# State-space prelude reordered: x projections first, taps read from PSUM, diagonals through DRAM, one residual moved to VectorE

## The chip, the cores and the metric

The kernel runs on 1 core of one Trainium2 chip. Its time is the device time of one execution in microseconds (us), from the first instruction to the last. Below, "batch 0" and "batch 1" are the two sequences of the input; all arithmetic here is fp32.

## The reference

Two layers, each a mixer and a mixture of experts, with adaptive layer norms around them. What the change touches is the first mixer, a state-space block over two sequences of 1024 tokens, 256 wide, 512 inner channels, 16 states, cut here to its core:

```
xz = h @ in_proj.T;  x, z = split(xz)                 # 512 + 512 channels
x = silu(conv over 4 taps of x, causal, + conv_b)
dt, B, C = split(x @ x_proj.T)                        # 16, 16, 16 columns
dt = softplus(dt @ dt_proj.T + dt_b)
h_t = h_(t-1) * exp(dt * A[n]) + dt * x * B_t[n]      # for 16 states n
y_t = sum over n of C_t[n] * h_t[n];   y = (y + x * D) * silu(z)
out = y @ out_proj.T
```

and, in the second layer's experts, `out = h + moe(rmsnorm(h))`, followed by `x = x + gb * out`. The term `gb * h` of that sum is the residual that the change moves to another engine.

## The kernel before, in words

The program is one sequence of stages: `modulation`, `mamba`, `moe` (layer 0), two attention stages, `moe` (layer 1). Each stage is a block with one hand-written instruction stream per engine; semaphores are its only ordering, so the order of calls in each stream is the schedule. Tiles have 128 partitions; 512 inner channels are CD = 4 chunks of 128 by L = 1024 tokens. The first number in a call like `conv(b, k)` is the batch and the second the chunk; the changed file numbers them i = 4b + k.

`mamba` has a prelude and a recurrence.

- **Prelude.** VectorE (DVE) normalises the rows of a batch (L424) and applies scale and shift (L427, L428). TensorE (PE) transposes them (`turned`, L652), ScalarE (ACT) copies the result out of PSUM to `hT` (`rows_of`, L522). PE makes the products of `projected` (L665), 16 half-chunks per batch: first the four x chunks, then the four z chunks; batch 0's z come ahead of batch 1's x. ACT copies each x half to `xp` (L536) and writes the fourth tap to `xc` (L541). `conv` on DVE adds the other three taps from `xp` (L433), `activated` (L527) makes silu of it: `xa`. `narrow` (L675) multiplies `xa` by `x_proj`; `split_xd` copies dt, B, C (L442). `steps` on PE (L693) makes the step sizes, `relu` (DVE, L452) and `absolute` (ACT, L561) their two halves, `falling` (Exp, L566) and `log1p` (Ln, L571) the softplus; `steps` on DVE sums them (L458) and multiplies by `xa` to `u` (L461).
- **What goes to DRAM.** `xa`, `z`, `dt`, `u` of each chunk (0.5 MB each) and the B and C rows are spilled by SyncE (SP), and read back before use. SP's stream is in program order: a wait in it holds all DMA issues behind it. For batch 0 the C values become 16 diagonal blocks `dg` of 128x1024 on GpSimd (POOL, L628), from columns that PE has transposed (L682); for batch 1 `place_words` (L342) writes the C values, 4 bytes each, onto the diagonals of a zeroed 8 MB table in DRAM (8 DMAs of 16x128 values, filled with zeros by L297), and `load_diag` (L369) reads that table back during the recurrence.
- **Recurrence.** 128 iterations, at = 16 kk + n, for 8 chunks kk of 16 states n. ACT: `decay` writes exp(dt A) to PSUM (L608). POOL: `dbx` = u times the broadcast B row, `bb` (L638; `load_rows`, L364). DVE: one scan (L496) over 1024 tokens into `h`. PE transposes `h` (L725) and sums over the states by a product with the diagonal block (L740). The first scans need `bb[0]` to be back from DRAM, the first sum needs `dg[0]`.

In `moe` of layer 1 POOL runs four instructions at the start (L925, L927: `res = hs * gb`, `x = x + res`, two groups of four rows). At the same time DVE finishes the statistics of the norm (`norm.spread`, L1286 to L1295), then waits for the norm's weights `nwb` (DMA, L882) and scales the rows (L1133).

Names of areas: `bb` and `dg` are 16 slots of 128x1024 each, `ud` four such slots, `xz`, `h`, `dbx`, `hts` two each. The prelude's temporaries lie in them: before the recurrence may load `bb[n]` or `dg[n]`, the temporary in that slot has to be done.

Of the kernel before, what the change touches and what calls it, by code (L numbers as in the profile page):

```python
# [7 lines left out]
P = 128  # L8
# [213 lines left out]
def mamba(nc, g, w_in, conv_w, conv_b, xproj, dtw, dtb, a_log, dskip, w_out):  # L222
    ctx = ExitStack()
    with ctx:
# [16 lines left out]
        ct = sb("ct", [P, TB * NS])  # L241

        xn = bb[:, 0:2, :].rearrange("p a (t d) -> p (a t) d", d=D)
        hT = [bb[:, 2:4, :], bb[:, 4:6, :]]
        win = bb[:, 6:8, :]
        xa = [bb[:, 8:12, :], bb[:, 12:16, :]]
        dtv, abs_v = [bb[:, 0:4, :], bb[:, 4:8, :]], [dg[:, 12:16, :], bb[:, 8:12, :]]
        zeros = dg[:, NS - 1, :]
        words = ud[:, :, :, :].rearrange("p a b l -> p (a b l)")
        XPW = L + DC - 1  # L250
        xp = words[:, 0:2 * XPW].rearrange("p (a l) -> p a l", a=2)
        wx = words[:, 2 * L + 64:2 * L + 64 + CD * 80].rearrange("p (k n) -> p k n", k=CD)
        wdt = words[0:DTR, 3 * L:3 * L + DI]
        xc, zr = h[:, :, :], xz[:, :, :]
# [28 lines left out]
        def dt_pair(b, k):  # L283

            return (3, 2, 0, 1)[k] if b == 1 else 3

        @block.sync
        def _(sp):
# [10 lines left out]
            def spill_z(b, k):  # L299
                sp.wait_ge(s_z, 2 * (b * CD + k) + 2)  # L300
                sp.dma_start(d_z[b * CD + k], zr[:, k % 2, :]).then_inc(s_zout[k % 2], 16)

            def spill_xa(b, k):
                sp.wait_ge(s_xa, b * CD + k + 1)
                sp.dma_start(d_xa[b * CD + k], xa[b][:, k, :]).then_inc(s_xaout[b], 16)

            def spill_rows(b):
                sp.wait_ge(s_xd, b + 1)
                sp.dma_start(d_b[b], xd[b][64:80, :]).then_inc(s_bout, 16)
                if b == 1:  # L310
                    sp.dma_start(d_c, xd[b][32:48, :]).then_inc(s_cout, 16)
# [2091 lines left out]
```

## Time and profile before

| | us |
|---|---|
| median of 3 runs (lowest, highest) | 2559.26 (2557.56, 2559.46) |
| the profiled execution | 2562.03 |
| its span, first to last instruction in the profile | 2560.2 |

The profile is one execution; times of its rows count from the start of the span. Whether something is on the path to the end of this single-core program is read stage by stage: the stages follow each other, and what an early stage ends sooner moves all later ones.

### The profile page before, as it was taken

The page shows a single profiled execution, that of the slowest core. Times are in us where ns is not written, and L with a number is a line of the kernel's source. Part 1 is how long each engine was busy: PE and PEld are TensorE (multiplying, and loading weights), DVE is VectorE, ACT ScalarE, POOL GpSimd, SP SyncE. Part 2 cuts the span into 40 slices and gives each one's busy share as a digit, 9 for nine tenths or more (in the row PEclk, how much of TensorE's full clock was granted, in tenths as well). Part 3 has the DMA queues.
Part 4 walks back from the last instruction along what each step waited for, and adds up shares of the span by engine and source line. Part 5 has one row for each costly group of instructions (what it writes and reads, how often), then busy time and mean ns, then how long its engine had stood idle before and what let it go on. Part 6 is the DMA issues. An engine that isn't in the chain of part 4 may idle for free. (4 is left out here: it accounts for less than half of the span.)

```text
span 2560.2 us, 34038 instructions
## 1 busy us (share of the span) xinstructions
PE 2337.4 (91%) x12526; PEld 1769.7 (69%) x12526; DVE 1416.2 (55%) x2477; ACT 1120.5 (44%) x1913; POOL 1140.2 (45%) x665
## 2 busy tenths in 40 slices
PE   6959999985999995999998989999999999949997
PEld 2329999983777764998896667777776777725554
DVE  5658888866222223545665875556556555463332
ACT  3467777722111112434433555546456464521221
POOL 0439999920332321433454445454545535223442
PEclk8969999997999997999998999999999999969999
DMA  6274181118412212000000100000000001055223
GB/s 243 83 284 114 58 329 59 64 73 267 133 30 34 32 26 98 1 1 1 1 1 19 56 1 19 15 10 19 1 23 1 19 9 34 1 175 145 45 42 64
DMA packets 108244, 168.30 MB, mean 66 GB/s; under 512 B 30482, under 2 KB 77586, under 8 KB 106004
## 3 DMA queue, kind: packets, MB, share of 16 engines
q1 hardware_dynamic: 93108, 145.35, 16.3%
q0 software_dynamic: 14976, 20.78, 5.1%
q8 instruction: 105, 1.72, 0.3%
q14 instruction: 55, 0.45, 0.1%
HBM read 115.94 MB, written 52.32 MB: 66 GB/s over the span
## 5 line engine op out<-in xcount | busy, mean ns | idle before, releaser
L638 POOL TENSOR_TENSOR mb_dbx<-mb_ud,mb_bb 128x1024 f32<-128x1024 f32 x128 | 302.0, 2363 | 57.2 <-DVE mb_h L496 41.7
L496 DVE TENSOR_TENSOR_SCAN mb_h<-ps,mb_dbx 128x1024 f32<-128x1024 f32 x128 | 292.2, 2289 | 47.9 <-ACT ps L608 37.5
L2298 PE MATMUL ps<-a_eT,a_v 128*128 128x512 f32 x576 | 297.2, 598 | 3.9 <-ACT a_eT L2175 3.9
L2131 POOL TENSOR_TENSOR a_e<-a_e,a_rc 128x1024 f32<-128x1024 f32 (+5 forms) x144 | 188.9, 1321 | 248.3 <-DVE a_rc L2047 247.9
L946 POOL DMA_INDIRECT e_acc<-e_hid,e_ids x78 | 123.6, 1585 | 370.8 <-DVE e_hid L1240 354.4
L2057 DVE TENSOR_REDUCE a_mx<-ps 128x1 f32<-128x1024 f32 (+7 forms) x256 | 192.7, 753 | 159.1 <-PE ps L2277 158.3
L2175 ACT ACTIVATE a_eT<-ps 128x512 f32<-128x512 f32 x288 | 171.1, 594 | 245.3 <-PE ps L2288 244.6
L740 PE MATMUL ps<-mb_dg,mb_hts 128*128 128x128 f32 x2048 | 251.2, 276 | 0.4
L740 PEld LDWEIGHTS ps<-mb_dg,mb_hts 128*128 128x128 f32 x2048 | 240.0, 193 | 1.9 <-issue 1.9
L1226 DVE COPY e_work<-ps 128x256 f32<-128x256 f32 x78 | 33.2, 425 | 356.4 <-PE ps L1064 356.4
L1803 POOL TENSOR_TENSOR a_elo<-a_e,a_ehi 128x1024 fp32r<-128x1024 f32 x48 | 117.6, 2451 | 223.2 <-ACT a_ehi L1656 117.7
L2159 ACT ACTIVATE a_e<-ps,a_nb 128x1024 f32<-128x1024 f32 (+5 forms) x192 | 156.0, 813 | 79.7 <-DVE a_nb L2058 72.9
L1095 PE MATMUL ps<-e_wd,e_work 128*128 (+1 forms) x780 | 189.0, 384 | 1.9 <-ACT e_work L994 1.9
L988 ACT ACTIVATE e_hid<-ps 128x688 f32<-128x688 f32 (+1 forms) x78 | 52.3, 670 | 299.8 <-PE ps L1076 299.8
L1076 PE MATMUL ps<-e_wg,e_work 128*128 x468 | 178.2, 518 | 4.7 <-issue 1.6
L617 ACT ACTIVATE mb_hts<-ps 128x512 f32<-128x512 f32 x256 | 139.3, 595 | 92.4 <-PE ps L725 92.4
L1076 PE MATMUL ps<-e_wu,e_work 128*128 x468 | 170.5, 500 | 0.0
L2274 PE MATMUL ps<-h_qkhi,h_wmhi 128*128 128x512 f32 (+3 forms) x288 | 152.7, 530 | 12.1 <-ACT a_e L2159 5.3
L725 PE MATMUL ps<-ident,mb_h 128*128 128x128 f32 x1024 | 135.4, 276 | 29.5 <-DVE mb_h L496 29.4
L1095 PEld LDWEIGHTS ps<-e_wd,e_work 128*128 128x128 f32 (+1 forms) x780 | 138.9, 190 | 30.0 <-issue 15.8
L2288 PE MATMUL ps<-ident,a_e 128*128 128x128 f32 x992 | 151.2, 275 | 8.2 <-DVE hs L2104 5.9
L2115 POOL TENSOR_TENSOR x<-x 128x1024 f32<-128x1024 f32 x35 | 91.0, 2601 | 135.8 <-DVE x L2090 135.8
(377 smaller groups left out, 5310.9 us busy)
## 6 DMA issues: line engine op xcount, KB each, us to landing
mb_bb<-mb_db_rows SPq DMA_DIRECT2D x16, 1024.0 KB, 12.6
mb_ddiag<-mb_dg SPq DMA_DIRECT2D x1, 8192.0 KB, 22.3
mb_dg<-mb_ddiag SPq DMA_DIRECT2D x8, 1024.0 KB, 14.0
e_wg<-in_g SPq DMA_DIRECT2D x8, 688.0 KB, 10.4
e_wu<-in_u SPq DMA_DIRECT2D x8, 688.0 KB, 10.7
e_wd<-in_d SPq DMA_DIRECT2D x8, 640.0 KB, 10.7
mb_dxa<-mb_bb SPq DMA_DIRECT2D x8, 512.0 KB, 2.6
mb_dz<-mb_xz SPq DMA_DIRECT2D x8, 512.0 KB, 2.9
```

Source lines behind the costliest of these rows:

```text
L496: dve.tensor_tensor_scan(h[:, at % 2, :], pair(at % 2), dbx[:, at % 2, :], 0.0, ALU.mult, ALU.add).then_inc(s_h, 1)
L638: pool.tensor_tensor(dbx[:, at % 2, :], ud[:, kk % 2, 0, :], bb[:, n, :], ALU.mult).then_inc(s_dbx, 1)
L740: mm = pe.matmul(ps[:, 6 + half, q * P:(q + 1) * P], hts[:, at % 2, c:c + P], dg[:, n, c:c + P], start=(n == 0 and q == 0), stop=(n == NS ...
L1076: mm = pe.matmul(ps[:, b0 + a, 0:FN], xT[:, i % 2, k * P:(k + 1) * P], w[:, ds(e), k, a * FN:(a + 1) * FN].rearrange("p a n -> p (a n)"), ...
L1095: mm = pe.matmul(ps[:, 6, 0:D], hT[0:n, i % 2, c * P:(c + 1) * P], wd[0:n, ds(e), c, :].rearrange("p a n -> p (a n)"), start=(c == 0), sto ...
L2057: own(dve.reduce_max(mx[:, q:q + 1], pair(n, (i + 1) * P), AX_X))
L2131: pool.tensor_tensor(probs(i, h), probs(i, h), rc[:, q:q + 1].to_broadcast([P, (i + 1) * P]), ALU.mult).then_inc(s["en"], 1)
L2159: act.activation(probs(i, h), pair(n, (i + 1) * P), ACT.Exp, bias=nb[:, q:q + 1], scale=SCALE, accum_out=sm[:, q:q + 1]).then_inc(s["e"], 1)
L2175: act.activation(eT[:, k % ER, :], ps[:, bank[what, u, i, h], :], ACT.Copy).then_inc(s["eT"], 1)
L2274: mm = pe.matmul(ps[:, o + t, 0:c1 - c0], qT[x_][j][:, i * P:(i + 1) * P], kT[y_][:, c0:c1], start=(x_ == y_), stop=(x_ == LO and not last))
L2288: tr = pe.transpose(ps[:, bank[token], h * P:(h + 1) * P], probs(i, h, j * P, (j + 1) * P), ident[:, :])
L2298: mm = pe.matmul(ps[:, 6 + rows[u, i] % 2, :], v[:, j, u % 2, :], eT[:, k % ER, :], start=(j == 0), stop=(j == i))
```

## The change

In `mamba`:

- Scale and shift leave DVE: PE transposes them to columns (`columns`), DVE copies these (`modT`), and ACT applies them in the eviction of the transposed rows.
- PE makes all x chunks first, with both narrow products between; batch 0's z come next, batch 1's z last, behind batch 1's step sizes. PSUM is handed out in four pairs of banks by the table `PAIR`.
- The copy `xp` is gone: ACT's tap and DVE's three taps read the product in PSUM.
- POOL's 16 diagonal products, the C columns and their copies are gone. `place_words` runs for both batches: for batch 0 in SP's prelude, for batch 1 behind all of batch 0's diagonal loads. `load_diag` runs for batch 0 too, 8 loads of 1 MB.
- Chunk 0's `dt` and `u` stay in `ud`; the first load of `ud` is gone.
- `z` has eight places: two of them are `dbx`, two are `h` (chunks 4 and 5). The first `dbx` waits for z 2 and 3 to be in DRAM, the first scan for z 4 and 5.

In `moe` of layer 1 the four residual instructions run on DVE, ahead of its wait for the logits.

```diff
-        zeros = dg[:, NS - 1, :]
+        zeros = dbx[:, 0, :]
+        zr = [xz[:, 0, :], xz[:, 1, :], dbx[:, 0, :], dbx[:, 1, :], h[:, 0, :], h[:, 1, :], xz[:, 0, :], xz[:, 1, :]]
...
+        PAIR = {"x": (2, 3, 0, 2, 3, 0, 2, 3), "dt": (1, 0, 1, 0, 2, 1, 0, 3), "z": (3, 1, 0, 3, 2, 1, 0, 3), "narrow": (1, 2)}
...
+            for k in range(CD):
+                spill_xa(0, k)
+            spill_xa(1, 0)
+            spill_rows(0)
+            spill_xa(1, 1)
+            place_words(0)
+            spill_xa(1, 2)
+            spill_xa(1, 3)
+            spill_z(0)
+            spill_z(1)
+            sp.wait_ge(s_tr, 4)
+            sp.wait_ge(s_dgout, 16 * TB)
+            load_diag(0, 0)
+            spill_z(2)
+            spill_z(3)
+            sp.wait_ge(s_ip, BK + CD)
+            load_diag(0, 1)
+            spill_rows(1)
+            for k in range(1, CD):
+                spill_steps(0, k)
+            sp.wait_ge(s_u, CD)
+            sp.wait_ge(s_bout, 16 * B)
+            load_rows(0, 0)
+            load_rows(0, 1)
+            sp.wait_ge(s_dtout[0], 16 * (CD - 1))
+            load_rows(0, 2)
+            load_rows(0, 3)
...
+            load_rows(0, 4)
+            load_rows(0, 5)
+            spill_steps(1, 0)
+            spill_steps(1, 1)
+            spill_z(4)
+            spill_steps(1, 2)
+            spill_z(5)
+            spill_steps(1, 3)
+            sp.wait_ge(s_log, BK)
+            sp.wait_ge(s_sp, BK)
+            load_diag(0, 2)
+            load_diag(0, 3)
...
             load_xz(0)
-            place_words()
+            for q in range(NS // 2):
+                sp.wait_ge(s_dgin[q], 16)
+            place_words(1)
...
-                    ins = dve.scalar_tensor_tensor(xc[:, k % 2, :], xp[:, k % 2, tap:tap + L], cw[:, k, tap:tap + 1],
-                                                   xc[:, k % 2, :], ALU.mult, ALU.add)
+                    late = DC - 1 - tap
+                    ins = dve.scalar_tensor_tensor(xc[:, i % 2, late:L], pair(PAIR["x"][i])[:, 0:L - late], cw[:, k, tap:tap + 1],
+                                                   xc[:, i % 2, late:L], ALU.mult, ALU.add)
...
+                if at == 0:
+                    dve.wait_ge(s_zout[2], 32)
                 if at >= 2:
                     dve.wait_ge(s_tp, 2 * (at - 1))
                 dve.tensor_tensor_scan(h[:, at % 2, :], pair(at % 2), dbx[:, at % 2, :], 0.0, ALU.mult, ALU.add).then_inc(s_h, 1)
...
+                if at == 0:
+                    pool.wait_ge(s_u, 1)
+                    pool.wait_ge(s_zout[1], 32)
...
-                if kk == CD and n % 2 == 0:
-                    pe.wait_ge(s_dgin[n // 2], 16)
+                if kk % CD == 0 and n % 2 == 0:
+                    pe.wait_ge(s_dgin[n // 2], 16 * (kk // CD + 1))
```

On SP, the place of the placed words (`mb_dxa` are spills of xa, `mb_dz` of z, `mb_ddt` and `mb_du` of dt and u; `mb_ddiag<-mb_dc_rows` are the placed words, `mb_bb<-mb_db_rows` the B rows, `mb_dg<-mb_ddiag` the diagonals). Before:

```order
L315 DMA mb_ddt<-mb_bb 128x1024
L317 DMA mb_du<-mb_bb 128x1024
L315 DMA mb_ddt<-mb_bb 128x1024
L317 DMA mb_du<-mb_bb 128x1024
L364 DMA mb_bb<-mb_db_rows 128x2048 x6
L349 DMA mb_ud<-mb_du 128x1024
L350 DMA mb_ud<-mb_ddt 128x1024
L357 DMA mb_xz<-mb_dxa 128x1024
L358 DMA mb_xz<-mb_dz 128x1024
L342 DMA mb_ddiag<-mb_dc_rows 16x128x1 x8
L349 DMA mb_ud<-mb_du 128x1024
```

Changed:

```order
L308 DMA mb_dxa<-mb_bb 128x1024 x4
L308 DMA mb_dxa<-mb_dg 128x1024
L312 DMA mb_dc_rows<-mb_hts 16x1024
L313 DMA mb_db_rows<-mb_hts 16x1024
L308 DMA mb_dxa<-mb_dg 128x1024
L327 DMA mb_ddiag<-mb_dc_rows 16x128x1 x8
L308 DMA mb_dxa<-mb_dg 128x1024 x2
L304 DMA mb_dz<-mb_xz 128x1024 x2
L362 DMA mb_dg<-mb_ddiag 128x2x1024
L304 DMA mb_dz<-mb_dbx 128x1024 x2
L362 DMA mb_dg<-mb_ddiag 128x2x1024
```

The eight placed-word DMAs stood behind all loads of B rows and the first loads of `ud` and `xz`; now they stand behind six spills of xa and the first C and B rows, and every spill of z, dt and u and every load of the recurrence is behind them.

Further down the same stream of the changed kernel, up to the spill of z 5:

```order
L356 DMA mb_bb<-mb_db_rows 128x2048 x6
L317 DMA mb_ddt<-mb_dg 128x1024
L319 DMA mb_du<-mb_dg 128x1024
L317 DMA mb_ddt<-mb_dg 128x1024
L319 DMA mb_du<-mb_dg 128x1024
L304 DMA mb_dz<-mb_h 128x1024
L317 DMA mb_ddt<-mb_dg 128x1024
L319 DMA mb_du<-mb_dg 128x1024
L304 DMA mb_dz<-mb_h 128x1024
```

The two `mb_dz<-mb_h` are z 4 and z 5, which the first scan waits for; six loads of B rows and six spills of dt and u stand ahead of the second.

In the second expert stage, POOL before:

```order
L1830 UNCONDITIONAL_BRANCH
L919 UNCONDITIONAL_BRANCH
L925 TENSOR_TENSOR e_scr<-hs,mod 128x1024
L927 TENSOR_TENSOR x<-x,e_scr 128x1024
L925 TENSOR_TENSOR e_scr<-hs,mod 128x1024
L927 TENSOR_TENSOR x<-x,e_scr 128x1024
L932 DMA e_xin<-e_rows,e_ids 128x264 x5
```

and DVE in the changed kernel, behind the scaled rows (L1170 is L1133 of the file before):

```order
L1170 SCALAR_TENSOR_TENSOR raw<-hs,n_rstd,e_nwb 128x256 x8
L1174 CAST raw<-e_cst 128x128
L1175 CAST raw<-e_cst 128x128
L1176 TENSOR_TENSOR e_gbd<-mod 128x256
L1177 MEMSET e_first 128x1
L1189 TENSOR_TENSOR e_scr<-hs,mod 128x1024
L1191 TENSOR_TENSOR x<-x,e_scr 128x1024
L1189 TENSOR_TENSOR e_scr<-hs,mod 128x1024
L1191 TENSOR_TENSOR x<-x,e_scr 128x1024
L1196 COPY e_hid<-ps 128x128
```

The four 128x1024 instructions stood at the head of POOL's stream, beside DVE's statistics, and stand now on DVE behind the scaled rows, ahead of the copy of the logits.

## Rows read from the trace of the kernel before

**Rows 1.** The page, part 1: busy time, share of the span, instructions of each engine.

```profile
PE 2337.4 (91%) x12526; PEld 1769.7 (69%) x12526; DVE 1416.2 (55%) x2477; ACT 1120.5 (44%) x1913; POOL 1140.2 (45%) x665
```

**Rows 2.** Timeline, 34 to 226 us: start us, us, engine, line, out<-in, count, [idle before].

```profile
42.33 0.26 ACT L514 ACTIVATE mb_am<-mb_am 128x64 f32<-128x64 f32 x1 [6.34 <-DMA mb_ud<-in_dtw]
...
51.58 0.34 PEld L665 LDWEIGHTS ps<-mb_bb 128*128 128x128 f32 x1 [0.52 <-issue]
...
52.74 0.19 PEld L665 LDWEIGHTS ps<-mb_bb 128*128 128x128 f32 x1 [0.24 <-issue]
...
95.02 1.22 DVE L442 COPY mb_hts<-ps 80x1024 f32<-80x1024 f32 x1 [23.88 <-PE ps L675]
...
179.80 4.46 DVE L496 TENSOR_TENSOR_SCAN mb_h<-ps,mb_dbx 128x1024 f32<-128x1024 f32 x2
185.85 4.47 DVE L496 TENSOR_TENSOR_SCAN mb_h<-ps,mb_dbx 128x1024 f32<-128x1024 f32 x2 [1.58 <-ACT ps L608]
...
199.03 2.29 DVE L496 TENSOR_TENSOR_SCAN mb_h<-ps,mb_dbx 128x1024 f32<-128x1024 f32 x1 [0.57 <-ACT ps L608]
...
225.63 2.29 DVE L496 TENSOR_TENSOR_SCAN mb_h<-ps,mb_dbx 128x1024 f32<-128x1024 f32 x1 [0.37 <-ACT ps L608]
```

**Rows 3.** Stretch 45 to 51 us: length, busy us of PE, PEld, DVE, ACT, POOL, granted clock, DMA.

```profile
45.00:51.00 6.00, 5.27 (x12) 2.83 (x11) 4.49 (x9) 1.60 (x4) 0.00 (x0) 0.50 1.03 416
```

**Rows 4.** Groups by line, 34 to 180 us: engine, operation, shapes, count | busy us, mean ns | idle.

```profile
L665 PE MATMUL ps<-mb_bb 128*128 128x512 f32 x128 | 66.1, 672 | 10.1 <-ACT mb_xz L551 8.2 <-issue 1.9
...
L693 PE MATMUL ps<-mb_hts,mb_ud 16*128 16x512 f32 x32 | 19.2, 747 | 2.9 <-ACT mb_dg L561 2.9
...
L452 DVE TENSOR_SCALAR mb_bb<-ps,mb_db 128x1024 f32<-128x1024 f32 x8 | 10.2, 1279 | 7.3 <-PE ps L693 7.3
...
L458 DVE TENSOR_TENSOR mb_bb<-mb_bb,mb_dg 128x1024 f32<-128x1024 f32 x4 | 4.9, 1220 | 3.3 <-ACT mb_dg L571 3.3
...
L522 ACT ACTIVATE mb_bb<-ps 128x512 f32<-128x512 f32 x8 | 4.5, 601 | 1.9 <-PE ps L652 1.8
```

**Rows 5.** Line 433 on VectorE, 50 to 75 us, then 98 to 125 us.

```profile
L433 DVE SCALAR_TENSOR_TENSOR mb_h<-mb_ud,mb_cw,mb_h x12: 1279/1285/1285, 55.3 to 69.9; 128x1024 f32<-128x1024 f32 x12
...
L433 DVE SCALAR_TENSOR_TENSOR mb_h<-mb_ud,mb_cw,mb_h x11: 1286/2814/2818, 97.5 to 123.3; 128x1024 f32<-128x1024 f32 x11
```

**Rows 6.** SyncE's DMA issues, 170 to 240 us, and landing times of line 342.

```profile
186.62 47.74 SPq L342 DMA_DIRECT2D mb_ddiag<-mb_dc_rows  x8
...
DMA to landing us min/median/max: 14.1/16.6/26.7
```

**Rows 7.** The page, part 6: DMA issues, count, KB each, us from issue to landing.

```profile
mb_ddiag<-mb_dg SPq DMA_DIRECT2D x1, 8192.0 KB, 22.3
```

**Rows 8.** DMA packets of all queues, 186 to 202 us, then 205 to 241 us.

```profile
DMA packets 1153, 6.68 MB, mean 418 GB/s; under 512 B 126, under 2 KB 126, under 8 KB 551
...
DMA packets 14105, 0.12 MB, mean 3 GB/s; under 512 B 14100, under 2 KB 14100, under 8 KB 14100
```

**Rows 9.** Timeline of the second expert stage's start, and the landing of line 882.

```profile
2248.72 2.34 POOL L925 TENSOR_TENSOR e_scr<-hs,mod 128x1024 f32<-128x1024 f32 x1 [33.70 <-POOLq L1830]
2248.73 2.35 DVE L1286 TENSOR_TENSOR n_mean<-n_st 128x8 f32<-128x8 f32 x1 [0.32 <-PEq L1830]
...
2249.56 0.46 SPq L882 DMA_DIRECT2D e_nwb<-in_n  x1
...
2251.12 0.17 DVE L1287 TENSOR_TENSOR n_t<-n_st 128x8 f32<-128x8 f32 x1
...
2251.32 2.19 DVE L1288 SCALAR_TENSOR_TENSOR n_t<-n_t 128x8 f32<-128x8 f32 x1
...
2258.77 3.25 DVE L1133 SCALAR_TENSOR_TENSOR raw<-hs,n_rstd,e_nwb 128x256 f32<-128x256 f32 x8
...
2275.29 0.29 DVE L1152 COPY e_hid<-ps 128x128 f32<-128x128 f32 x1 [8.44 <-PE ps L1032]
...
DMA to landing us min/median/max: 5.7/5.7/5.7
```

More of the change, by code:

```diff
@@ L464, in _ @@
             normalised(1)
[L465 to L480 removed]
+            for i in range(6):
+                conv(i)
@@ L482, in skip @@
+            relu(0)
+            conv(6)
+            relu(1)
+            conv(7)
+            relu(2)
+            relu(3)
+            dve.wait_ge(s_dbl, 2)
+            dve.tensor_copy(xd[1], flat(ps[0:80, 2 * PAIR["narrow"][1]:2 * PAIR["narrow"][1] + 2, :])).then_inc(s_xd, 1)
+            for i in range(CD, BK):
+                relu(i)
+            for i in range(BK):
+                steps(i)
             def skip(kk):
@@ new lines, in gate @@
+            def gate(i):
+                act.wait_ge(s_ip, BK + i + 1)
+                if i == 0:
+                    act.wait_ge(s_zfill, 16)
+                    act.wait_ge(s_xa, BK)
+                if i == 6:
+                    act.wait_ge(s_zout[0], 32)
+                act.activation(zr[i], pair(PAIR["z"][i]), ACT.Silu).then_inc(s_z, 1)
+            rows_of(0)
+            tap(0)
+            tap(1)
+            activated(0)
+            tap(2)
+            rows_of(1)
+            activated(1)
@@ new lines, in _ @@
+            tap(3)
+            activated(2)
+            tap(4)
+            activated(3)
+            tap(5)
+            activated(4)
+            act.wait_ge(s_dbl, 1)
+            act.activation(xd[0], flat(ps[0:80, 2 * PAIR["narrow"][0]:2 * PAIR["narrow"][0] + 2, :]), ACT.Copy).then_inc(s_xd, 1)
+            tap(6)
+            activated(5)
+            absolute(0)
+            tap(7)
+            activated(6)
+            absolute(1)
+            activated(7)
+            absolute(2)
+            gate(0)
@@ L710, in _ @@
-            narrow(1)
-            projected(1, 12, 14)
-            projected(1, 14, 16)
-            for k in range(CD):
-                steps(1, k)
-            pe.wait_ge(s_abs, BK)
-            pe.wait_ge(s_relu, BK)
+            inner(3)
+            inner(4)
+            narrow(0, 0)
+            narrow(0, 1)
+            inner(5)
+            narrow(0, 2)
+            narrow(0, 3)
+            inner(6)
+            steps(0)
+            inner(7)
+            steps(1)
+            narrow(1, 0)
@@ L718, in turn_state @@
+            narrow(1, 1)
+            steps(2)
+            gated(0)
+            narrow(1, 2)
+            steps(3)
+            gated(1)
+            narrow(1, 3)
+            gated(2)
+            gated(3)
+            for i in range(CD, BK):
+                steps(i)
+            for i in range(CD, BK):
+                gated(i)
+            pe.wait_ge(s_z, BK)
             def turn_state(at):
@@ L1147, in _ @@
                 ins.then_inc(s_xn, 1)
+            if hs is not None:
+                for r in range(NG // B, NG):
+                    four = slice(4 * r, 4 * r + 4)
+                    own(dve.tensor_tensor(res[:, four, :], hs[:, four, :],
+                                          over(mod[:, r // (NG // B), GB * D:(GB + 1) * D], 4), ALU.mult))
+                    ins = dve.tensor_tensor(x[:, four, :], x[:, four, :], res[:, four, :], ALU.add)
+                ins.then_inc(s_res, 1)
             col = lambda ap: ap.rearrange("p (e j) -> p e j", e=EXP)
```

413 lines of the change are left out of this document (172 added, 241 removed).

## The prediction

> **What bounds the kernel now.** I read the page first: PE is busy 91% of the span, no other engine above 55% [rows 1]. That is a mean over stages, so I went on to the stages that the change touches, and there the answer is another. The timeline of the prelude and the recurrence [rows 2] shows PE start its first product after 42.9 us, batch 0's dt, B, C arrive at 95.0, and the first scan of the recurrence at 179.8. The scans begin slowly: numbers 0 and 2 are 6.05 us apart, number 6 comes only at 199.03, because B rows are late from DRAM, and from there each takes 2.66 us (ten from 199.03 to 225.63). So scan 16, at 225.63, is the mark: everything behind it keeps its length, and what is gained is the amount by which it comes earlier. Before the first scan the bound is a chain over engines, PE busy with 66.1 us of products [rows 4] while DVE's taps take 1.28 us each in batch 0 and up to 2.82 in batch 1 [rows 5], when POOL builds diagonals. Then I read SP's queue and the DMA: placing the words kept SP 47.7 us [rows 6], at a place where nobody waited for it. In `moe` the timeline shows small DVE instructions of 2.2 us beside POOL's [rows 9].
>
> **The compute side of the prelude.** It becomes much shorter. PE cannot start its products before ACT's am instructions (42.33, twice 0.26 us [rows 2]) and four evictions of 0.60 [rows 4]: 45.4. A product of one chunk is 8 records. While the granted clock is 0.50, the 1.2 GHz level, as in 45 to 51 us behind an idle stretch [rows 3], a record comes every 0.34 + 0.52 = 0.86 us, later, at 2.4 GHz, every 0.19 + 0.24 = 0.43 [rows 2]: 6.9 or 3.44 us. I take the first product slow: 52.3. Two more: 59.2. Batch 1's transposes with their waits, an estimate of 3.3: 62.5. Three products and four narrow steps (4 records each, 1.75 us) make 17.3: 79.8. The C values are in SBUF at 81. The seventh product ends at 83.2, its tap and the silu of chunk 1 of batch 1, each about two of the 0.60 us halves, at 85.7; that spill stands ahead of the words in SP's stream, so the words begin at 86.1. DVE keeps up if a tap from PSUM costs what a tap from SBUF does. A tap from PSUM is not in the trace. Its nearest row is the relu, which reads 1024 values from PSUM in 1.28 us [rows 4], the same as an undisturbed tap; the other end is the 2.82 us of the disturbed ones [rows 5]. I take 1.28, as it is the same memory and POOL is now silent. PE's rest is ten products (34.4 us), eight step sizes (19.2 us as they are now [rows 4]) and four narrow steps (7.0): 140 at the earliest, about 144 with a wait for ACT. The last gate, a table load and the decay end at about 150 (estimate). Before, the first scan was at 179.8. On this side alone 25 to 30 us would be gained: z of batch 0 no longer delays batch 1's x, scale and shift leave DVE, and the doubled taps go.
>
> **The DMA side of the prelude.** It takes most of that back. One placed-word DMA writes 16 x 128 = 2,048 words. Between 205 and 241 us, when little else moved, 14,100 small packets went out in 36 us [rows 8], 392 per us, so 5.2 us for one DMA and 41.8 for eight, at 3 GB/s: bytes do not limit them. Until now the recurrence hid them; that cover is gone. SP's stream is in order and so is the data behind it. Queue time: 87.4 (behind the last spill of xa) + 41.8 = 129.2. Then come, ahead of the landing of z 5: two xa and z 0 to 3 (3 MiB), diagonals 0 and 1 (2), dt and u of batch 0's chunks 1 to 3 (3), six loads of B rows (6), dt and u of batch 1's chunks 0 to 2 (3), z 4 and 5 (1): 18 MiB. Their rate lies between 418 GB/s [rows 8] and 8 MiB in 22.3 us, 376 GB/s [rows 7]. I take 410, 2.56 us per MiB, since the first is a long mixed stretch and the second includes a landing: 46.2 us, and 1.3 to land. The first scan writes the slot of z 4 and 5 and waits for them: **176.7**. That is 27 us after its inputs are ready, yet 3.1 before the 179.8 of today. From then on B rows are there: the last pair needed in time, rows 12 and 13, is 9 MiB behind z 5, 199.7, for a use at about 203. Diagonal 4 lands at 182, for a use near 190. Scan 16: 176.7 + 16 x 2.66 + 0.7 for a slow first pair, as now (6.05 against 5.32) = 220.0. **Gain 5.6 us.** Batch 1's words start at about 206 and hold SP to about 242, for loads used after 260: nothing.
>
> Here a rule of the Trainium skill speaks against the change. The row shows 5.2 us for 8 KB. *DMA: Bandwidth & Descriptors*, Rules for kernel authors, says that a strided last dimension becomes one descriptor per element and should be rearranged; its table of measured bandwidth puts a packet at about 10.5 ns of an engine. By that estimate 16,384 words on 16 engines are 11 us, not 42, and the sum would be that of the first rival. The trace has a duration, so the trace's is used.
>
> Deleted POOL work costs and gains nothing by itself beyond the taps: the 16 diagonal blocks were off the chain. The eight added diagonal loads are in the sum above or behind z 5. The eight transposes of the modulation and a 128x8 copy lie before 45.4, beside ACT's wait.
>
> **The residual on VectorE.** Four of DVE's small instructions, each while one of POOL runs, take 2.2 to 2.35 us, one between two of POOL's takes 0.17 [rows 9]; without POOL 4 x 2.1, 8.3 us, go. But the next step waits for `nwb`: issued at 2249.56, landed 5.7 later, 2255.3, where DVE now arrives at 2258.77 [rows 9]. **Gain 3.5 us**; between 0, if the weights land later among the expert weights, and 8.3. The four instructions on DVE, 1.22 us each [rows 4], fill part of the 8.44 us in which it idles before 2275.29 [rows 9]; without that cover they would cost 4.9.
>
> **Sum.** 5.6 + 3.5 = 9.1 us. The profiled execution took 2562.0 (span 2560.2), so the changed kernel's would take 2552.9. The median shown, 2559.3, is 2.8 lower; against it: **2550.2 us**, 0.36% less. About 0.2%, 5.1 us, is what a measurement of this kernel can tell from no change.
>
> **The rivals.**
>
> 1. *The words are cheap.* If their slow pace came from the work beside them, eight could take 20 us or less. For it: 3 GB/s is far from what the engines can move [rows 8]. Against: 36 us at one mean rate while the loads were done. Then the B rows wait for u of batch 0 at about 135; ten MiB and a landing later, 163, the first scan starts. Scan 16 at 207: 18.8 + 3.5 = 22.3 us faster, **2537**. Chance 0.18.
> 2. *The words are dearer, and the kernel is slower.* Place: SP's queue between the first C rows and diagonal 0. SP was held 47.7 us, and a landing takes 14.1 to 26.7 us behind the issue [rows 6]. I read the landing as overlapping the next issues. If both add up, 47.7 + 17, the words end at 152 instead of 129: 23 us later against 9.1 gained, 14 slower, **2573**. It decides from 51 us for the eight, 6.3 each. With SP's 47.7 alone (6.0 each) the gain is 3.2, **2556**. Chance of over 6.3: 0.10. A tap from PSUM at 2.82 us would have the same sign: six convolutions ahead of the words at 8.5 in place of 3.9, 27 us later, **2577**; 0.03.
> 3. *The prelude moves nothing.* Bulk at 376 GB/s adds 4.1 us, a word phase of 44 adds 2: the two recurrences start alike and only `moe` is left, 3.5 us, **2556**. Nothing in the rows speaks against the slow rate but the longer stretch at 418. Chance 0.17.
>
> The forecast, the queue deciding with a gain of over 5.1, has 0.52.
>
> **The numbers.** Faster by over 0.2%: forecast and rival 1, 0.70, less 0.02 for `moe` giving nothing: 0.68. Within 0.2%: 0.20. Slower: 0.12. The range goes from rival 1's 2537 to 2562, the slow bulk rate together with the dear words (6.0 each) and no gain in `moe`.
>
> **What would show it.** In the profile of the changed kernel: C rows of batch 0 issued near 81 us; eight word DMAs from about 86, SP free near 121, diagonal 0 issued near 130; taps of 1.28 us; ACT's first decay before 152 and the first scan at 177 with the DMA of z as its releaser; scans 2.66 us apart with no gap at numbers 2 to 6. In `moe` the statistics in 0.2 us each, then a wait for `nwb`. It is wrong if the first scan follows its decay at once (rival 1), if the words end after 138 (rival 2), if taps exceed 1.5 us, or if a sum over states waits for a diagonal.

## The result, and the profile after

| | us | ratio to the kernel before, 95% interval |
|---|---|---|
| the change, first comparison (19 runs) | 2567.16 (2558.27 to 2578.72) | 1.0032 (1.0022 to 1.0042) |
| the kernel before beside it (19 runs) | 2559.35 (2555.45 to 2564.41) | |
| the change, second comparison (11 runs) | 2560.02 (2552.49 to 2569.04) | 1.0003 (0.9991 to 1.0014) |
| the change, third comparison (12 runs) | 2558.84 (2553.10 to 2564.97) | 0.9999 (0.9988 to 1.0010) |
| profiled execution of the change (first comparison) | 2564.84, span 2563.0 | |

The forecast was 2550.2, 0.36% faster. The first comparison says 0.32% slower, outside the range; the two later ones say no difference. None shows a gain, so the forecast of one is wrong, and in the first comparison its sign too. Of the 7.8 us between the two medians of the first comparison the two profiles show only 2.8; the rest has no profile. The times of the changed kernel also scatter over 12 to 20 us in a comparison, those of before over 7 to 11.

The busy times moved as the change says [rows 1]: VectorE 26 us less, GpSimd 50 less.

```profile
PE 2331.9 (91%) x12526; PEld 1768.7 (69%) x12526; DVE 1389.9 (54%) x2475; ACT 1112.5 (43%) x1890; POOL 1090.7 (43%) x645
```

VectorE's timeline of the recurrence in the changed kernel, to be laid beside [rows 2]. Its line 516 is line 496 of before, and `x2` stands for two scans.

```profile
181.05 4.47 DVE L516 TENSOR_TENSOR_SCAN mb_h<-ps,mb_dbx 128x1024 f32<-128x1024 f32 x2 [32.17 <-DMA mb_dz<-mb_h]
187.10 4.47 DVE L516 TENSOR_TENSOR_SCAN mb_h<-ps,mb_dbx 128x1024 f32<-128x1024 f32 x2 [1.58 <-ACT ps L623]
192.27 2.29 DVE L516 TENSOR_TENSOR_SCAN mb_h<-ps,mb_dbx 128x1024 f32<-128x1024 f32 x1 [0.70 <-ACT ps L623]
...
224.19 2.29 DVE L516 TENSOR_TENSOR_SCAN mb_h<-ps,mb_dbx 128x1024 f32<-128x1024 f32 x1 [0.37 <-ACT ps L623]
...
265.40 2.29 DVE L516 TENSOR_TENSOR_SCAN mb_h<-ps,mb_dbx 128x1024 f32<-128x1024 f32 x1 [0.37 <-ACT ps L623]
274.41 4.59 DVE L516 TENSOR_TENSOR_SCAN mb_h<-ps,mb_dbx 128x1024 f32<-128x1024 f32 x2 [6.71 <-POOL mb_dbx L650]
```

The first scan waits 32.17 us for the spill of z into DRAM, as forecast. The scans then run at 2.66 us without the early gaps of before, and scan 16 comes at 224.19, 1.4 us ahead of the 225.63 of before. But the last row is new: scan 32, the first of the third chunk, waits 6.71 us for GpSimd. In the kernel before it came at 269.51. GpSimd's own rows say what it waited for:

```profile
157.61 4.63 POOL L650 TENSOR_TENSOR mb_dbx<-mb_ud,mb_bb 128x1024 f32<-128x1024 f32 x2 [121.93 <-DMA mb_bb<-mb_db_rows]
...
271.98 4.64 POOL L650 TENSOR_TENSOR mb_dbx<-mb_ud,mb_bb 128x1024 f32<-128x1024 f32 x2 [7.17 <-DMA mb_ud<-mb_ddt]
```

And SP's rows, the counterpart of [rows 6], say why the dt of chunk 2 was late (L327 are the placed words, batch 0's and batch 1's; L341 and L342 load u and dt):

```profile
80.90 0.32 SPq L312 DMA_DIRECT2D mb_dc_rows<-mb_hts  x1
...
85.90 37.47 SPq L327 DMA_DIRECT2D mb_ddiag<-mb_dc_rows  x8
...
133.71 0.37 SPq L362 DMA_DIRECT2D mb_dg<-mb_ddiag  x1
...
147.42 8.24 SPq L356 DMA_DIRECT2D mb_bb<-mb_db_rows  x6
...
162.25 2.24 SPq L304 DMA_DIRECT2D mb_dz<-mb_h  x1
...
202.91 50.81 SPq L327 DMA_DIRECT2D mb_ddiag<-mb_dc_rows  x8
253.83 4.73 SPq L341 DMA_DIRECT2D mb_ud<-mb_du  x1
258.61 3.13 SPq L342 DMA_DIRECT2D mb_ud<-mb_ddt  x1
```

Batch 1's words held SP from 202.91 to 253.72. Before, they held it from 186.62 to 234.36, and the same load was issued at 234.47:

```profile
234.47 6.32 SPq L349 DMA_DIRECT2D mb_ud<-mb_du  x1
```

Now it is issued 19 us later, and dt needs 13.4 us more to land (258.61 to about 271.98), behind the last words. Everything behind keeps that: the next stage's first load is issued at 577.22, against 570.91. The second expert stage then gives 3.0 us back: from its first statistics to the end it takes 308.5 us, where it took 311.5. The balance of the two profiles is 6.3 - 3.0 = 3.3, less 0.5 in the stages between the first mixer and that point, and the spans differ by 2.8.

In that stage, against [rows 9]:

```profile
2254.53 0.17 DVE L1330 TENSOR_TENSOR n_mean<-n_st 128x8 f32<-128x8 f32 x1 [0.32 <-PEq L1874]
...
2254.94 0.17 DVE L1332 SCALAR_TENSOR_TENSOR n_t<-n_t 128x8 f32<-128x8 f32 x1
...
2261.95 3.25 DVE L1170 SCALAR_TENSOR_TENSOR raw<-hs,n_rstd,e_nwb 128x256 f32<-128x256 f32 x8 [5.63 <-DMA e_nwb<-in_n]
...
2278.26 0.29 DVE L1196 COPY e_hid<-ps 128x128 f32<-128x128 f32 x1 [3.44 <-PE ps L1069]
```

The statistics take 0.17 us each, then VectorE waits for the norm weights, as forecast; the logits are copied 23.7 us behind the first statistic, where it was 26.6.

The pace of the words, from the packets of all queues: the changed kernel in batch 0's words (92 to 122 us) and in batch 1's (215 to 245 us).

```profile
DMA packets 10606, 0.07 MB, mean 2 GB/s; under 512 B 10604, under 2 KB 10604, under 8 KB 10604
```

```profile
DMA packets 8306, 0.07 MB, mean 2 GB/s; under 512 B 8304, under 2 KB 8304, under 8 KB 8304
```

That is 353 and 277 packets a us. The prediction took 392 from [rows 8] for both.

In neither stretch were the DMA engines full. This is SP's queue in the first one, 92 to 122 us (packets, MB, share of the time of 16 engines):

```profile
q1 hardware_dynamic: 10604, 0.04, 17.1%
```

17.1% of 16 engines over 30 us, divided by 10,604 packets, is 7.7 ns of one engine for each word of 4 bytes. All 16,384 words are then about 8 us of the 16 engines, spread over more than 40. What sets the pace between the packets no run here shows.

### The profile page after: what moved, and what is told of

Read it like the earlier page. It is cut to its first block and busy times, and to the rows that moved or that the text cites. A ratio compares the mean times of both kernels' runs of the same rounds, so it can differ in the third digit from the quotient of the medians.

```text
span 2563.0 us, 34007 instructions
## 1 busy us (share of the span) xinstructions
PE 2331.9 (91%) x12526; PEld 1768.7 (69%) x12526; DVE 1389.9 (54%) x2475; ACT 1112.5 (43%) x1890; POOL 1090.7 (43%) x645
## 3 DMA queue, kind: packets, MB, share of 16 engines
q1 hardware_dynamic: 111252, 151.77, 17.1%
## 5 line engine op out<-in xcount | busy, mean ns | idle before, releaser
L969 POOL DMA_INDIRECT e_xin<-e_rows,e_ids x78 | 76.9, 986 | 188.2 <-DVE e_ids L1259 164.8
## 6 DMA issues: line engine op xcount, KB each, us to landing
mb_ddiag<-mb_dbx SPq DMA_DIRECT2D x1, 8192.0 KB, 23.7
e_wu<-in_u SPq DMA_DIRECT2D x8, 688.0 KB, 10.7
e_wd<-in_d SPq DMA_DIRECT2D x8, 640.0 KB, 10.5
```

## The experiments

**Residual alone.** The kernel before with only the residual moved, out of GpSimd's stream and into VectorE's ahead of its wait for the logits:

```diff
-                for r in range(NG // B, NG):
...
-                    pool.tensor_tensor(x[:, four, :], x[:, four, :], res[:, four, :], ALU.add).then_inc(s_res, 1)
...
+                for r in range(NG // B, NG):
...
+                    ins = dve.tensor_tensor(x[:, four, :], x[:, four, :], res[:, four, :], ALU.add)
```

> The kernel before with only the residual of the second expert stage on VectorE. Theory (the stage gives 3 us back, the loss is all in the first mixer): the mixer ends where it ended, 570.9 us, the small statistics of VectorE take 0.17 us each, then a wait for the norm weights of some 5 us, and the time is 3.0 us below the kernel before (ratio 0.9988). Rival (the residual costs what it takes on VectorE): 4 x 1.22 us appear behind the scaled rows and the copy of the logits comes no earlier: no gain or up to 2 us slower.

Measured: 2556.13 us, ratio 0.9987 (0.9978 to 0.9996). The time fits, the profile doesn't. The mixer ended at 563.4, though its code is that of before; and the last stretch took 311.6 us, with no gain, though the statistics were fast. TensorE's matmuls of the router in this run, and in the changed kernel:

```profile
2254.71 3.10 PE L1017 MATMUL ps<-e_work,e_rw 128*8 128x512 f32 x4
...
2258.78 1.88 PE L1017 MATMUL ps<-e_work,e_rw 128*8 128x512 f32 x4
```

```profile
2267.09 1.88 PE L1061 MATMUL ps<-e_work,e_rw 128*8 128x512 f32 x4
```

The granted clock in the 4 us of the first router products, first this run, then the changed kernel (length, busy us of PE, PEld, DVE, ACT, POOL, clock, DMA):

```profile
2254.66:2258.66 4.00, 4.00 (x13) 1.24 (x12) 3.97 (x12) 1.67 (x3) 0.00 (x0) 0.68 0.36 125
```

```profile
2267.53:2271.53 4.00, 4.00 (x16) 1.31 (x14) 3.97 (x11) 2.42 (x5) 0.00 (x0) 1.00 0.48 163
```

At 0.68 the four products take 3.10 us, at 1.00 they take 1.88. So part of what the residual gains can be lost to TensorE's clock behind its idle stretch. The trace shows where the rest went. Counted from the first statistic, this run is ahead of the kernel before by 2.4 us at the scaled rows (7.7 against 10.0), by 1.1 at the logits (25.5 against 26.6), and by 0.4 when ScalarE takes the first expert product out of PSUM (57.2 against 57.6). TensorE came out of an idle stretch there once more, at a granted clock of 0.57 in the six us around it (2293 to 2299), where it was 0.67 in the kernel before (2301 to 2307). The last 0.3 us go later in the stage. That the clock did it is read from these rows; no run set it.

**Words of batch 1 in pairs.** `place_words` here takes as its second argument which of the eight blocks of words it writes:

```diff
-            place_words(1)
+            place_words(1, (0, 1))
             for kk in range(1, BK):
...
                 elif kk + 1 < BK:
                     load_ud(kk + 1)
+                if kk < CD:
+                    place_words(1, (2 * kk, 2 * kk + 1))
                 load_xz(kk)
```

> The changed kernel with batch 1's eight word DMAs cut into four pairs: one pair where all eight stood, one pair in each of the next three chunks, behind the load of the step sizes that is due there. Theory (the mixer lost 7.75 us between scan 16 and the third chunk because SP was held 50.8 us, from 202.9 to 253.7, and the load of chunk 2's dt landed only at about 271.9): the wait of 7.2 us on GpSimd at scan 32 is gone, the mixer ends at about 569.5 in place of 577.2, and the time is 7.7 us below the changed kernel, about 2559.5 by the medians, the same as before. Rival (the loss is in the landing times, whatever stands ahead): the wait only moves to a later chunk and the mixer still ends after 575.

Measured: 2559.03 us, ratio 0.9993 (0.9984 to 1.0001). The wait at scan 32 is gone, the load for chunk 2 is issued at 220.31:

```profile
200.10 9.69 SPq L327 DMA_DIRECT2D mb_ddiag<-mb_dc_rows  x2
...
220.31 0.33 SPq L341 DMA_DIRECT2D mb_ud<-mb_du  x1
220.69 1.46 SPq L342 DMA_DIRECT2D mb_ud<-mb_ddt  x1
222.24 4.34 SPq L327 DMA_DIRECT2D mb_ddiag<-mb_dc_rows  x2
```

and the mixer ends at 566.5. The wait is gone in this run and in its repeat. The mixer of the change also has a profile without a wait (table below), so the firmer proof that the block of words makes it is the pair in the order of need, further down: 10.7 us against none. What it is worth on average this run alone does not say, since the changed kernel was not timed beside it; that came last.

**z ahead of the B rows.**

```diff
+            spill_z(4)
+            spill_z(5)
             sp.wait_ge(s_u, CD)
             sp.wait_ge(s_bout, 16 * B)
             load_rows(0, 0)
...
             spill_steps(1, 1)
-            spill_z(4)
             spill_steps(1, 2)
-            spill_z(5)
```

> The changed kernel with the spills of z 4 and z 5 ahead of all loads of B rows on SP. Theory (the first scan waits for the landing of z 5, behind 18 MiB at 2.56 us each): 9 MiB are left ahead of it, so z 5 lands near 157, the first scan starts when the first B rows have landed and one product on GpSimd is done, near 162 in place of 181. The queue carries the same bytes, so the last B rows, number 7, land near 209 and the last diagonals near 204: waits appear at scans 12 to 15, and scan 16 is at about 217 instead of 224.2, 7 us earlier. The words of batch 1 still hold SP, so the third chunk still waits, and the whole is 0 to 7 us faster than the changed kernel. Rival (the first scan is bound by compute): it stays above 175.

Measured: 2559.23 us, ratio 0.9992 (0.9978 to 1.0005).

```profile
159.64 4.61 DVE L516 TENSOR_TENSOR_SCAN mb_h<-ps,mb_dbx 128x1024 f32<-128x1024 f32 x2 [11.31 <-POOL mb_dbx L650]
...
189.28 2.29 DVE L516 TENSOR_TENSOR_SCAN mb_h<-ps,mb_dbx 128x1024 f32<-128x1024 f32 x1 [8.14 <-ACT ps L623]
...
202.65 4.59 DVE L516 TENSOR_TENSOR_SCAN mb_h<-ps,mb_dbx 128x1024 f32<-128x1024 f32 x2 [3.09 <-POOL mb_dbx L650]
...
268.56 4.59 DVE L516 TENSOR_TENSOR_SCAN mb_h<-ps,mb_dbx 128x1024 f32<-128x1024 f32 x2 [11.91 <-POOL mb_dbx L650]
```

The first scan comes 21 us earlier, so z was what held it. The gaps at scan 8 (TensorE waited 5.36 us for diagonal 2, which I had not listed) and at scan 12 take back half of it; scan 16 is at 213.1. The wait at the third chunk then grows to 11.9: an earlier mixer meets the same late load.

**No words for batch 0** (batch 0's sums over states are left out, its diagonals being zeros).

```diff
-            place_words(0)
```

> The changed kernel without batch 0's eight word DMAs: batch 0's outputs of the state sums are then left out (its diagonals are zeros). Theory (the queue behind the words decides): the words took 5.1 us each, 41 us in all, and without them the first scan starts when its inputs are computed and the first B rows can be loaded, so at 155 to 160 in place of 181: 21 to 26 us of the 41, since the compute side is ready only at 150. Scan 16 at 198 to 203, and the whole 21 to 26 us below the changed kernel, or a few more where the second word phase is no longer late for the third chunk. Rival (the words cost little and bytes or compute decide): first scan above 170.

Measured: 2545.50 us, ratio 0.9943 (0.9929 to 0.9957), 21.7 us below the changed kernel's first median, but 13 to 15 below its two later ones (2560.02 and 2558.84). Diagonal 0 is issued at 108.26 in place of 133.71, and

```profile
166.06 4.47 DVE L515 TENSOR_TENSOR_SCAN mb_h<-ps,mb_dbx 128x1024 f32<-128x1024 f32 x2 [13.44 <-DMA mb_dz<-mb_h]
```

The first scan is 15 us earlier and not 21 to 26: z 4 and 5 still stand behind the B rows. Scan 32 still waits, 3.3 us, and the mixer ends at 559.3.

**The order of need.** Behind batch 1's C and B rows SP's stream is written anew, with the same waits; `spill_steps(1, k)` falls apart into its dt and its u, and the order ends with B rows 5, the four u, B rows 6, diagonal 5, B rows 7, diagonals 6 and 7, z 6, z 7, u and dt of chunk 1:

```diff
+            spill_z(4)
+            spill_z(5)
...
             load_rows(0, 0)
             load_rows(0, 1)
+            for k in range(CD):
+                sp.wait_ge(s_sp, CD + k + 1)
+                sp.dma_start(d_dt[CD + k], dtv[1][k]).then_inc(s_dtout[1], 16)
...
             load_rows(0, 2)
...
+            load_diag(0, 2)
             load_rows(0, 3)
+            load_diag(0, 3)
...
             load_rows(0, 4)
...
+            load_diag(0, 4)
             load_rows(0, 5)
```

> The changed kernel with SP's stream behind batch 1's C and B rows put in the order in which the recurrence needs things: z 4 and 5, B rows 0 and 1, dt of batch 1, B rows 2, diagonal 2, B rows 3, diagonal 3, and so on; the last two z go last. The bytes and the words are the same. Theory (with the words done near 129, 29 MiB at 2.56 us each end near 204 in any order, and only the order decides who waits): first scan at 158 to 162 as with z first (159.6 there), no waits of over 3 us at scans 2 to 14, scan 16 near 203 to 207 in place of 224.2. The words of batch 1 hold SP about 50 us from about 195, and the third chunk still waits, the longer by what the scans are earlier: about 11.9 us as with z first or more, up to 25. So of the 18 us most are lost again, and the whole is 5 to 10 us below the changed kernel, as with z first (2559). Rival (the order gains what it seems to): 18 us, 2549.

Measured: 2562.47 us, ratio 1.0003 (0.9994 to 1.0012).

```profile
211.93 4.59 DVE L518 TENSOR_TENSOR_SCAN mb_h<-ps,mb_dbx 128x1024 f32<-128x1024 f32 x2 [4.82 <-POOL mb_dbx L652]
...
268.42 4.59 DVE L518 TENSOR_TENSOR_SCAN mb_h<-ps,mb_dbx 128x1024 f32<-128x1024 f32 x2 [10.70 <-POOL mb_dbx L652]
```

Scan 16 came at 211.9 and not at 203 to 207, since I had left the load of chunk 1's dt last (4.82 us of wait). The rest was lost at the third chunk, as expected.

> The same order, and batch 1's word DMAs in four pairs. Theory: scan 16 near 203 to 207, no wait at the third chunk, the mixer ends near 548 in place of 577; 2567 less 7.7 for the spread words less 18 for the order is 2541, 2538 to 2545. Rival (the two gains are the same gain): about 2551.

Measured on the same chip: 2548.71 us, ratio 0.9947 (0.9934 to 0.9960), 13.8 us below the same order with the words in one block. Scan 16 is as before at 211.8, but scan 32 has no wait and the mixer ends at 557.7. This pair shows what holding SP for eight word DMAs costs once the scans are early.

**Residual back on GpSimd.** The changed kernel, with the expert stage of before, twice.

> The changed kernel with the residual back on GpSimd. Theory A (the residual gives 3.0 us through the statistics of VectorE): from the first statistics of the second expert stage to the end 311.5 us as in the kernel before, in place of 308.5, and the time is 3 us above the changed kernel. Theory B (in the run with the residual alone this stretch was 311.6: TensorE's granted clock behind its idle stretch, 0.68 there and 1.00 in the changed kernel, decides as much as the residual): the stretch is between 309.5 and 311.5, with the logits 1 to 3 us later than the 23.7 us behind the statistics of the changed kernel.

> The changed kernel with the residual back on GpSimd, once more, beside the changed kernel on the same chip. The first time its ratio to the kernel before was 1.001, lower than the 1.003 of the changed kernel, although the second expert stage was 3 us longer (311.2 against 308.5 us to the end). Theory (that was the scatter of the words): on one chip it comes out 0 to 5 us above the changed kernel, and its last stretch is 311 us again. Rival (the residual on VectorE costs time elsewhere): it comes out 4 us below again.

Measured: 2562.96 us, ratio 1.0010 (1.0001 to 1.0018), and 2562.22, ratio 1.0009 (0.9998 to 1.0020). The last stretch took 311.2 and 311.4 us. On one chip with the changed kernel the second came out 2.2 us above it, with intervals that overlap. So the times agree with theory A and do not show it alone; the profiles do: 3.0 us is what the residual is worth. The same stretch took 308.0 to 308.8 us in eleven profiles with the residual on VectorE, and 311.2 to 311.7 in the four with it on GpSimd; the residual alone, 311.6, is the one exception.

**Batch 0's words from GpSimd's queue.**

In GpSimd's stream behind its memset, with a semaphore of its own that SP's first load of a diagonal waits for:

```diff
             pool.memset(zeros, 0.0).then_inc(s_zero, 1)
...
+            pool.wait_ge(s_zfill, 16)
+            pool.wait_ge(s_cout, 16)
...
+                for q in range(TB):
+                    pool.dma_start(flat_dg[:, q * P:q * P + (P - 1) * (L + 1) + 1:L + 1],
+                                   d_c[0, :, q * P:(q + 1) * P]).then_inc(s_dgp, 16)
...
-            place_words(0)
...
-            sp.wait_ge(s_dgout, 16 * TB)
+            sp.wait_ge(s_dgp, 16 * TB)
             load_diag(0, 0)
```

> The changed kernel with batch 0's eight word DMAs issued by GpSimd, which is idle from 36 to 157 us, and not by SP. The bulk transfers then need not stand behind them. Theory A (a small packet holds its DMA engine, so words and bulk share 41 + 46 us of the same engines): the last word lands later than 129, the first scan stays at 175 to 185, scan 16 at 218 to 228. Theory B (a small packet mostly waits, and the engine could serve another queue meanwhile): the spills pass the words, z 5 lands near 157 and the first scan starts at 155 to 165. Either may be spoiled by the issue on GpSimd: if it builds the descriptors at under 392 packets a us the words end after 129, and VectorE's taps of 1.28 us may become as slow as 2.8, as they were beside GpSimd's products.

Measured: 2548.47 us, ratio 0.9950 (0.9937 to 0.9963).

```profile
82.39 7.47 POOL L643 DMA_DIRECT2D mb_ddiag<-mb_dc_rows  x7 [47.01 <-DMA mb_dc_rows<-mb_hts]
...
112.82 1.04 POOL L643 DMA_DIRECT2D mb_ddiag<-mb_dc_rows  x1 [22.96 <-issue]
```

```profile
84.44 11.82 SPq L308 DMA_DIRECT2D mb_dxa<-mb_dg  x3
99.89 7.58 SPq L304 DMA_DIRECT2D mb_dz<-mb_xz  x2
120.68 0.37 SPq L362 DMA_DIRECT2D mb_dg<-mb_ddiag  x1
```

The issue costs GpSimd 8.5 us of idle time. The words are done by 120.68, when diagonal 0 is issued, 13 us earlier than in the changed kernel, and spills of xa and z went beside them; the first scan is at 168.04, scan 16 at 211.6. Scan 32 waits 1.6 us, and the mixer ends at 557.9. GpSimd's queue between 84 and 120 us, in the terms of the row of SP's queue above:

```profile
q0 software_dynamic: 384, 0.07, 32.3%
```

Bulk and words can share the time, so theory B is nearer; that SP's words filled only 17% of the engines' time says the same of the changed kernel. How far it goes is open: only 2.6 MB stood beside the words here.

**All three edits together.** The two edits above and the words of batch 1 in pairs; here the spills of z 0 to 3 also go ahead of diagonal 0, z 6 and 7 ahead of B rows 6, and u and dt of chunk 1 ahead of diagonal 7:

```diff
+            for k in range(1, CD):
+                spill_xa(1, k)
+            for i in range(CD):
+                spill_z(i)
             sp.wait_ge(s_tr, 4)
             sp.wait_ge(s_dgp, 16 * TB)
             load_diag(0, 0)
...
             load_diag(0, 6)
+            load_ud(1)
             load_diag(0, 7)
```

> The three edits together: batch 0's words issued by GpSimd, SP's stream in the order of need (all spills of xa and z that are ready go ahead of diagonal 0), batch 1's words in four pairs. Theory (the queue decides, and words beside the spills cost it little): z 5 lands near 150, the first scan starts at 150 to 156, scans 2.66 us apart, scan 16 at 193 to 200 in place of 224.2, no wait at the third chunk, the mixer ends near 542 and the time is 2528 to 2536. Rival (what GpSimd's words gained was the order and the spreading's gain once more): about 2546, as each of the two had alone.

Measured: 2528.65 us (2527.31 to 2531.59), ratio 0.9879 (0.9864 to 0.9893). The first scan no longer waits for any DMA:

```profile
151.57 4.46 DVE L516 TENSOR_TENSOR_SCAN mb_h<-ps,mb_dbx 128x1024 f32<-128x1024 f32 x2
...
186.45 4.60 DVE L516 TENSOR_TENSOR_SCAN mb_h<-ps,mb_dbx 128x1024 f32<-128x1024 f32 x2 [2.76 <-POOL mb_dbx L657]
...
196.93 2.29 DVE L516 TENSOR_TENSOR_SCAN mb_h<-ps,mb_dbx 128x1024 f32<-128x1024 f32 x1 [0.37 <-ACT ps L623]
```

The mixer ends at 540.6. This is the compute side of the prelude that the prediction had ready at 150, collected; it beats both kernels, the one before by 31 us. Scan 16 comes 27 us earlier than in the three profiles of the mixer before, whose mean is 223.6, and the residual gives the 3.0 us of above.

**Repeats.** The changed kernel and the kernel before once more, then the changed kernel beside the spread words.

> The changed kernel itself, once more, for a second profile and a time beside the other three of this call. Two profiles of the same first mixer differ: with its own residual the changed kernel's first scan came at 181.1 and its third chunk waited 6.7 us; with the residual of before, at 176.0 and no wait. Theory (the pace of the words changes from run to run): here too the mixer ends anywhere between 563 and 577, and 0 or up to 8 us are lost at the third chunk, as the loads of dt of chunk 2 land before or after about 270. Against the kernel before: ratio 1.000 to 1.004. Rival (the loss belongs to this kernel's instruction streams, whatever the run): a wait of 6 to 8 us again, the mixer ends at 577 and the ratio is 1.003.

> The kernel before itself, for a second profile and for the noise of the comparison. Expected: ratio within 0.1% of 1; first scan between 174.0 and 179.8, as in the two profiles so far of its first mixer, which differed by the granted clock of TensorE between 40 and 60 us (0.50 and 0.89, or 0.73 and 1.00); the mixer ends between 563 and 571, and never with a wait at the third chunk; 311.5 us from the first statistics of the second expert stage to the end.

> The changed kernel, beside the spread words on the same chip. Its ratio to the kernel before was 1.0032 at first and 1.0003 the second time; the wait at the third chunk was 6.7 and 3.2 us in the two profiles. Theory (the slow pace of batch 1's words makes that wait, and the wait makes the difference): a ratio of 1.000 to 1.004, and 2 to 8 us above the kernel with the spread words; the wider range of its times (20 us, and 17 the second time, against 9 to 10 for the kernel before) shows again. Rival (the wait is an accident of two profiles): the two kernels of this call come out within 1 us.

> Batch 1's words in four pairs, once more, beside the changed kernel. Theory: ratio to the kernel before 0.998 to 1.000, no wait at the third chunk, a range of about 10 us, and 2 to 8 us below the changed kernel of this call. Rival: within 1 us of it.

The kernel before: 2560.17 us, ratio 0.9998 (0.9990 to 1.0007). The spread words, beside the changed kernel's 2558.84: 2556.04, ratio 0.9987 (0.9978 to 0.9996), 2.8 us below it, with no wait at scan 32. That is in the range of the theory, at its low end; the two intervals still overlap. The profiles of the two mixers, in us:

| profile | first scan | scan 16 | wait at scan 32 | mixer ends | SP held by words, batch 0 and 1 |
|---|---|---|---|---|---|
| before | 179.8 | 225.6 | none | 570.9 | none, 47.7 |
| before, again | 179.7 | 225.4 | none | 570.8 | none, 46.5 |
| residual alone (mixer of before) | 174.0 | 219.8 | none | 563.4 | none, 44.5 |
| changed | 181.1 | 224.2 | 6.7 | 577.2 | 37.5, 50.8 |
| changed, again | 179.4 | 223.4 | 3.2 | 572.6 | 36.7, 47.5 |
| changed, third | 179.1 | 222.3 | 2.5 | 567.8 | 36.7, 46.8 |
| residual back (mixer of the change) | 176.0 | 219.8 | none | 563.4 | 33.6, 47.5 |
| residual back, again | 178.6 | 221.8 | 1.1 | 567.6 | 34.1, 43.4 |

By the means, the changed mixer reaches scan 16 1.3 us earlier and ends 1.3 us later. With the 3.0 us of the residual that makes a gain of 1.7, too small for these comparisons to tell from nothing, and two of the three say no difference. The first, 0.32% slower, was on another occasion; its profile has the longest wait, and its highest times reach 2578.7. Whether all its runs had slow words is not known, since only one of them was profiled.

The time for which the words hold SP does not order the waits by itself: 47.5 us went once with a wait of 3.2 and once with none. The issue of chunk 2's dt does. It ended at 261.7, 258.4, 258.0, 255.8 and 250.1 in the five profiles with waits of 6.7, 3.2, 2.5, 1.1 us and none.

## Why the prediction was wrong

By its own steps:

- **The compute side held.** C rows at 80.9 us (forecast 81), words from 85.9 (86.1), taps from PSUM 1.279 us (1.28), the first decay at 148.0 (before 152). That it would bring nothing by itself held as well: 33 us lay between that decay and the first scan.
- **The queue behind batch 0's words held within 4 us.** SP was free at 123.4 (121), diagonal 0 went out at 133.7 (130), the first scan came at 181.05 (176.7) with z as its releaser. Five profiles lie between 176.0 and 181.1, mean 178.8: the mean is 2.1 us late, and batch 0's words went at 353 to 409 a us where the term took 392. Rival 1, words in 20 us or less, fell with it: at 353 to 409 a us 16,384 words take 40 to 46 us. The prediction's estimate of 11 us, from the packet time in the Trainium skill (*DMA: Bandwidth & Descriptors*, Measured), is not the time that passes either. That page of the Trainium skill has 10.5 ns as the 0.67 us of a 4 KB load divided by its 64 packets; that it is the time of one engine was my reading. The trace has 7.7 ns of an engine for each word, near that figure; but the engines were busy for 17% of the time, so it did not decide.
- **"Batch 1's words ... hold SP to about 242, for loads used after 260: nothing" failed.** This is the step that took back what was left. I had costed a hidden edit by the time of its issues alone. The words can start only when the bulk ahead of them has gone, in this trace near 209. At the 392 a us of [rows 8] they end 16,384 / 392 = 42 us later, at 251, and 1 MiB of u and dt lands by about 255. The use is at 264.8, where GpSimd's wait begins (271.98 less 7.17). So the cover was 10 us wide, and I never worked it out. Measured: 277 a us; at that pace 59 us, so words to 268; dt at about 272, and the wait. Between scan 16 and the end of the mixer the first profile lost 7.7 us, and the mean of five lost 2.6, where the sum had nothing. In all five profiles of the changed mixer batch 1's words were slower than in the three of before (277 to 349 against 385 to 458), which I can't explain.
- **The 5.6 us at scan 16 were 1.4** in the pair of profiles: the 4.3 us by which z landed late, and nothing else. What the pair hides is that the mixer of before is no fixed length: another profile of the same code has scan 16 at 219.8. By the means the 1.4 are 1.3. This term is mis-sized by 4.3 us, the most of any by the means: the changed mixer reached scan 16 at 222.3 and not at 220.0, and the mixer before at 223.6 and not at the 225.6 of the one profile that the prediction had. So the 9.1 us of the sum became 1.3 + 3.0 - 2.6 = 1.7.
- **The residual held:** 3.0 us for 3.5, with the norm weights as the next wait.
- **Rival 2 named the right resource and the wrong place.** It had SP held by words between the first C rows and diagonal 0; it was SP held by words ahead of chunk 2's dt. Its limit of 6.3 us for each DMA was not the limit there: the first profile has 50.8 / 8 = 6.35, but with 46.8 / 8 = 5.85 a wait of 2.5 us was left.
- **The top of the range was added wrongly.** The slow bulk rate (4.1 us), words at 47.7 us (5.9) and no gain in `moe` give 5.6 - 4.1 - 5.9 = -4.4, so 2563.7 and not 2562. The 2567.16 lies outside both.

## What to carry to other kernels

A queue in program order is a resource with due times, like an engine. When a change lets a long block of issues start later or run twice, take the first load behind *each* place of the block, work out when it lands and not only when it is issued, and compare that with its use; a margin under the scatter of the block's pace is no cover. When a prelude gets shorter on the compute side and nothing happens, look at the order in which the transfers were put behind each other: here the same bytes in the order of need, with the slow ones on a second queue or cut into pairs, gave 28 of the 31 us; the other 3 are the residual's.

## What the hardware showed that I had not expected

- One and the same mixer came out 5.9 us longer or shorter at scan 16, and 7.5 at its end, and TensorE's granted clock at its start differed with it. Between 40 and 60 us, the kernel before and the residual alone, whose code is the same there:

```profile
40.00:50.00 10.00, 6.50 (x20) 4.58 (x21) 6.16 (x11) 2.90 (x6) 0.00 (x0) 0.50 1.03 397
50.00:60.00 10.00, 10.00 (x22) 4.30 (x21) 8.43 (x6) 6.06 (x8) 0.00 (x0) 0.89 1.02 412
```

```profile
40.00:50.00 10.00, 6.94 (x25) 4.83 (x26) 6.44 (x10) 3.50 (x7) 0.00 (x0) 0.73 1.02 407
50.00:60.00 10.00, 10.00 (x25) 4.50 (x24) 9.82 (x8) 8.36 (x10) 0.00 (x0) 1.00 1.02 410
```

  The first is at 1.2 GHz for the whole of the first ten us, the second not; batch 0's dt, B, C are there at 95.0 and at 90.7, the first scan at 179.8 and at 174.0. The repeat of the kernel before had 0.50 and 0.90 there and its first scan at 179.7. Three profiles are too few to say that the clock is all of it.
- The stages between the first expert stage's start and the second's statistics take either 1677 to 1679 us or 1681 us, in kernels with the same code there. The reason is open.
- GpSimd issued seven DMAs of 2,048 words in 7.5 us, where SP was held 33 to 51 us for eight. Between 84 and 120 us the trace has 384 packets of its queue, far fewer than words, but their 0.07 MB are all the words (16,384 x 4 bytes). So a packet of this queue holds about 43 words, and by the 32.3% it takes 0.48 us of an engine, 11 ns for each word. From the first issue to diagonal 0 the words took 38 us (82.4 to 120.7), with 2.6 MB of spills beside them; from SP they took 48 (85.9 to 133.7).
